# Scan stage of an eight-layer kernel: the second block's depthwise convolution on TensorE with diagonal tap matrices instead of on VectorE

## The reference, cut to what matters

```
xc, z  = split(x @ in_proj.T)
xt     = depthwise_conv(xc, conv_w, 4 taps, causal, zeros ahead of each sequence) + conv_b
xs     = silu(xt)
dt, B, C = split(xs @ x_proj.T);  dt = softplus(dt @ dt_proj.T + dt_b)
h[t]   = exp(dt[t] * A) * h[t-1] + dt[t] * B[t] * xs[t]        # per channel and state
y      = (sum over states of h * C + D * xs) * silu(z)
out    = y @ out_proj.T
```

## Time and profile before

| what | value |
|---|---|
| median of 3 runs | 4525.6 us (4520.05 to 4526.73) |
| the profiled execution, own time | 4532.35 us |
| its span in the trace | 4530.6 us |
| busy: PE, DVE, ACT, POOL | 3978.4, 3387.8, 2843.7, 2065.0 us |
| scan stage starts (input norm rows) | about 1639 us |
| step 0: first scan to first scan of step 1 | 1676.05 to 1839.87 us |

### The profile page before, as it was taken

The page is one execution under the profiler, slowest core; times in us unless marked ns, Lnnn a source line. Parts: engine busy times, 40 slices in busy tenths (PEclk is TensorE's granted clock), DMA queues, the critical chain, the costliest instruction groups (busy, mean ns, idle before and its releaser), DMA issues. The chain is left out here.

```text
span 4530.6 us, 106618 instructions
## 1 busy us (share of the span) xinstructions
PE 3978.4 (88%) x39260; PEld 2174.0 (48%) x39268; DVE 3387.8 (75%) x5857; ACT 2843.7 (63%) x4508; POOL 2065.0 (46%) x1885
## 2 busy tenths in 40 slices
PE   8899999887859842599999999999988999999888
PEld 4344444554637520244545445455453555555555
DVE  8899999565654469888888888885146888888586
ACT  3577777554443236688887888875124666667664
POOL 5122222331224559888888788885011222222312
PEclk9899999889978975799999999999998999999999
DMA  4211111015324434355555655654223212222100
GB/s 137 64 37 39 36 37 39 12 43 114 62 98 122 108 108 104 104 164 143 150 159 153 163 138 150 174 149 130 83 74 103 70 55 58 57 65 59 31 10 29
DMA packets 263622, 411.22 MB, mean 91 GB/s; under 512 B 52636, under 2 KB 139708, under 8 KB 263076
## 3 DMA queue, kind: packets, MB, share of 16 engines
q1 hardware_dynamic: 233480, 376.07, 29.4%
q0 software_dynamic: 6912, 18.88, 1.7%
q10 hardware_dynamic: 22848, 11.02, 1.2%
HBM read 351.85 MB, written 53.24 MB: 89 GB/s over the span
## 5 line engine op out<-in xcount | busy, mean ns | idle before, releaser
L992 DVE CUSTOM_DVE_ANT_0 banks<-banks,l3s_table 128x1024 f32<-128x1024 f32 x512 | 620.0, 1240 | 126.9 <-PE banks L912 121.7
L1073 ACT ACTIVATE l3s_probs<-banks 128x512 f32<-128x512 f32 x1024 | 542.4, 595 | 256.3 <-PE banks L912 139.0
L2688 POOL TENSOR_TENSOR l_dbx<-l_u,l_bc 128x1024 f32<-128x1024 f32 x256 | 602.8, 2355 | 178.6 <-DVE l_u L3093 62.0
L987 DVE TENSOR_REDUCE l0s_peak<-banks 128x1 f32<-128x1024 f32 x512 | 604.7, 1212 | 59.5 <-PE banks L912 59.1
L1073 ACT ACTIVATE l0s_probs<-banks 128x512 f32<-128x512 f32 x1024 | 536.1, 600 | 174.1 <-PE banks L912 172.4
L2698 POOL TENSOR_TENSOR l_ys<-l_ys,l_hc 128x1024 f32<-128x1024 f32 x232 | 547.3, 2359 | 40.7 <-DVE l_hc L3113 36.4
L2929 ACT ACTIVATE banks<-l_dt,l_decay 128x512 f32<-128x512 f32 x512 | 345.4, 686 | 218.7 <-DVE banks L3102 215.5
L2826 PE MATMUL banks<-l_ha,l_ring 128*128 128x512 f32 x1024 | 446.6, 593 | 0.1
L2826 PE MATMUL banks<-l_hb,l_ring 128*128 128x512 f32 x1024 | 442.9, 593 | 1.6 <-DMA l_ring<-in_l2f_stream 1.6
L912 PE MATMUL banks<-l3s_q_st,l3s_k_st 122*32 122x512 bf16 x4096 | 359.5, 385 | 32.4 <-issue 22.4
L3102 DVE TENSOR_TENSOR_SCAN banks<-banks,l_carry,l_dbx 128x512 f32<-128x512 f32 x256 | 329.4, 1288 | 76.0 <-ACT banks L2929 49.5
(11 more groups left out here) (499 smaller groups left out, 7271.8 us busy)
## 6 DMA issues: line engine op xcount, KB each, us to landing
l_bc<-l_bc_rows SPq DMA_DIRECT2D x256, 512.0 KB, 5.3
l_ring<-in_l2f_stream SPq DMA_DIRECT2D x176, 512.0 KB, 6.5
l3s_table<-bias_table SPq DMA_DIRECT2D x16, 960.0 KB
y_rows<-l1f_out_b SPq DMA_DIRECT2D x80, 128.0 KB
qk_parts<-l0q_q_parts SPq DMA_DIRECT2D x48, 128.0 KB
qk_parts<-l0q_k_parts SPq DMA_DIRECT2D x48, 128.0 KB, 2.4
l0s_q_st<-qk_parts SPq DMA_DIRECT2D x64, 96.0 KB
l0s_k_st<-qk_parts SPq DMA_DIRECT2D x64, 96.0 KB
```

Source lines behind the costliest of these rows:

```text
L987: nc.vector.tensor_reduce(out=peak[:, b % 2, t:t + 1], in_=s1[t % 2], axis=AX, op=ALU.max, negate=True).then_inc(s1_used, 1)
L992: nc.vector.tensor_tensor_reduce(out=s1[t % 2], in0=s1[t % 2], in1=rows, scale=1.0, scalar=LOW, op0=ALU.add, op1=ALU.max, accum_out=peak[: ...
L1073: nc.scalar.activation(columns(probs[b % 2][:, t, :], half * 512, (half + 1) * 512), scores, ACT.Exp, scale=scale).then_inc(s2_used, 1)
L2688: nc.gpsimd.tensor_tensor(dbx[:, at:at + 2], u[:, 2 * mh:2 * mh + 2], bc[:, load % BR, 0].unsqueeze(1).to_broadcast([P, 2, TB]), ALU.mult)\
```

## The change

The convolution of block 1 alone, whose input is taken in step 0, is made by TensorE. In the prologue, between taking the turned rows and `take_x(0, 0)`, ScalarE builds 16 matrices of 128x128 float32 (four taps, four channel groups), each the identity scaled per row by a tap. They lie in `ha`, which the perceptron fills only from step 1 on. In step 0, TensorE, after the four input projections and ahead of the projection to dt, B and C, makes four matmuls of 128x512 per group, one per tap, with the diagonal as the stationary matrix and the shifted `xc` as the moving one, accumulating in the group's bank. `take_x` for block 1 is then the copy alone; the bias goes into silu's own bias operand. VectorE makes no convolution in step 0; the reset of the first three columns moves from behind unit 42 to behind unit 46, ahead of `gated`, with a wait for the four convolutions. Blocks 0 and 2 to 7 are as before.

```diff
+        diagonals = ha[:, 0:TAPS, :].rearrange("p j (c m) -> p j c m", m=P)
...
+            def convolve_second(c):
+
+                bank = place[f"in1.{c}"][0]
+                pe.wait_ge(tap_done, CT + c + 1)
+                for j in range(TAPS):
+                    last = nc.tensor.matmul(banks[:, bank, :], diagonals[:, j, c, :], xc[:, c, j:j + TB],
+                                            start=(j == 0), stop=(j == TAPS - 1))
+                last.then_inc(conv_ready, 1)
...
+                    if q == AT["xp_pe"] and n == 0:
+                        pe.wait_ge(diagonals_ready, 1)
+                        for c in range(CT):
+                            convolve_second(c)
                     if q == AT["xp_pe"] and more:
                         project_dbl(n + 1)
...
+                if n == 1:
+                    nc.scalar.activation(xc[:, i, TAPS - 1:], banks[:, bank, :], ACT.Copy).then_inc(tap_done, 1)
+                    return
                 nc.scalar.activation(xc[:, i, TAPS - 1:], banks[:, bank, :], ACT.Copy)
...
-                nc.scalar.activation(xs[n % 2][:, i, :], banks[:, bank, :], ACT.Silu).then_inc(taken[bank], 1)
+                offset = {"bias": conv_b[:, i:i + 1]} if n == 1 else {}
+                nc.scalar.activation(xs[n % 2][:, i, :], banks[:, bank, :], ACT.Silu, **offset).then_inc(taken[bank], 1)
...
             act.wait_ge(first_loaded, 16 * 3)
+            for j in range(TAPS):
+                for c in range(CT):
+                    last = nc.scalar.activation(diagonals[:, j, c, :], chip.ident[:], ACT.Copy, scale=taps[:, c, j:j + 1])
+            last.then_inc(diagonals_ready, 1)
             for i in range(CT):
                 take_x(0, i)
...
                     for i in range(CT):
-                        if k == AT["conv"][i] and more:
+                        if k == AT["conv"][i] and n and more:
                             convolve(n + 1, i)
+                    if n == 0 and k == AT["xs"][CT - 1]:
+                        v.wait_ge(conv_ready, 2 * CT)
+                        nc.vector.memset(xc[:, :, 0:TAPS - 1], 0.0).then_inc(xc_kept, 1)
```

More of the change, by code:

```diff
@@ L2491, in scan_and_mlp @@
         tap_done, conv_ready, xc_kept = s.sem("tap_done"), s.sem("conv_ready"), s.sem("xc_kept")
+        diagonals_ready = s.sem("diagonals_ready")
         skip_done = s.sem("skip_done")
```

## The result

The changed kernel takes 4538.3 us (median of 13 runs, 4533.3 to 4542.1) against 4526.7 us for the kernel before on the same chip (13 runs, 4520.1 to 4529.5). The ratio is 1.0026, 95% interval 1.0018 to 1.0033. It is 12 us slower where 3 us faster was forecast, and the forecast range ended at 4531. The profiled execution took 4538.82 us, its span is 4537.0.

The account below looks back on a forecast made before the run. GpSimd was taken to bound step 0, with VectorE limiting only beside convolutions. Step 0's -4.0 us and the prologue's +0.8 gave -3.2, from 4525.6 to a median of 4522.4 us, range 4514 to 4531.

Parts of the forecast that it names:

- What bounds step 0: Step 0: GpSimd sets the pace, 4.61 us per pair against VectorE's 3.95; its 6.32 us of idle pieces can be had.
- Term A: Step 0: GpSimd's gaps waiting for a scan or product by C close once VectorE's convolutions go, gaining 4.0 us.
- The gap at `gated` stays: End of step 0: GpSimd's 2.46 us gap remains, as VectorE operations with two SBUF inputs and GpSimd's take turns.
- Term B: Prologue: ScalarE's 16 diagonals take 4.67 us where 3.88 are free, so `take_x(0, 0)` starts 0.8 us late.
- B counts in full: Prologue: the 0.8 us delay from building diagonals passes wholly to the first scan, as everything up to it hangs on `take_x(0, 0)`.
- TensorE's cost 0: Step 0: convolution groups of 4.4 to 8.1 us delay silus too little to matter; cost 0, bounds 0 and 5 us.
- VectorE's waits for GpSimd: Step 0, units 30 to 46: VectorE's idle time before scans grows from one 0.70 us wait to 5 to 6 us.
- Later steps are as before: After step 0: nothing changes; diagonals are read before step 1 writes `ha`, GpSimd and transfers keep their order.
- the change touches only these 200 us: Start of prediction: only the 200 us holding prologue and step 0 are affected; what they gain or lose passes on.
- a slower time for a reason that no row shows: Whole kernel: a slower outcome from a cause not visible in the profile rows, chance 0.03.

Follow-up runs that it names:

- k = 16: Kernel before plus 16 tiny bf16 matmuls on TensorE ahead of block 1's first projection, VectorE's convolution kept: 4546.7 us against 4536.1, ratio 1.0024.

## Why the prediction was wrong, step by step

**What bounds step 0: right.** GpSimd did, and its idle pieces were what could be had. With VectorE freed by 9.7 us the step gains 3.8.

**Term A, -4.0 us: right, -3.77.** The product behind `gated` was forecast at 1790.6, it came at 1790.58 (shifted). All 3.86 us of gaps closed. Later 0.28 us is lost at one scan that waits 1.44 us for its exponential, before 1.16. Over all traces step 0 takes 163.8 us with VectorE's convolution (163.79 to 163.85, nine traces) and 159.8 to 160.1 with TensorE's (six).

**The gap at `gated` stays: right.** It is 2.46 us as before, although VectorE reaches its multiplication earlier: at 1779.32, 0.2 us before GpSimd starts its add at 1779.52. It now takes 3.63 us in place of 2.23 and ends 1.1 us behind that add (1781.87). The two take turns.

**Term B, +0.8 us: right at the copy, wrong in what it costs.** The 16 diagonals took 4.78 us where 4.67 were forecast, and the first copy of `xc` comes 0.79 us late. But "B counts in full" did not hold. VectorE's convolution ends 0.56 us late, then TensorE's last products of the projection to dt, B and C are done so much sooner (ScalarE waits 1.19 us for them in place of 1.75), and the first scan is not late at all in this pair. From first projection to first scan the five kernels with diagonals in the prologue take 31.40 to 31.46 us and the ten others 31.04 to 31.46, on average 0.2 us less. The granted clock in the last 2.5 us ahead of that copy is 0.84 in place of 0.78, which fits; why it is higher is open. The scan stage alone would have given -3.8, not -3.2.

**TensorE's cost 0: right.** The groups took 3.60 to 6.37 us, and the third silu starts 8.52 us behind its copy's end, as before. Three scans wait 0.2, 1.2 and 0.2 us for an exponential behind a silu; GpSimd shows no gap there, so they cost nothing.

**VectorE's waits for GpSimd: mis-sized.** I forecast one wait of 0.70 us to grow to 5 to 6 us. Four waits of 0.67 to 0.78 came, 3.0 us, and 1.6 us for ScalarE.

**"Later steps are as before": this is the step that failed.** It was argued from data and order: same instructions, same waits, same transfers. The same assumption stands at the start of the prediction, "the change touches only these 200 us". It left out that 65 instructions more stand in TensorE's stream, so that all later code of that engine lies elsewhere against the packets in which it is fetched. In a loop of 3912 instructions this moved the end of the first packet behind each back-jump from 83 to 18 instructions. That cost 2.7 us a pass, 13.7 in all, over three times the gain. The profile of the kernel before had the sign: "PE banks L912 <- issue" with five waits of over 4 us, in a loop with five back-jumps. I had read the profile only near the change. I had given 3 in 100 to a slower time for a reason that no row shows; a row did show where such a reason could act.

What is shown and what is not: that position alone makes and unmakes the loss is shown, by the same loss without convolution, by its absence with padding, and by its absence without jumps. That the second packet is late, and not something else at the same instruction, rests on the place of the stall, which moves with the padding instruction for instruction (18, 20, 52), and on the trace's own record of each packet. At all 60 back-jumps of the twelve kernels that have them, a packet of 16 KB lands 1.5 to 1.8 us ahead of TensorE's resumption. The next one starts to move only 0.4 to 1.6 us after the resumption. At all 20 second stalls it is this one that lands 1.2 to 1.7 us ahead of their end. At the second jump of the changed kernel: stop at 3711.28, packet from 3713.05 to 3714.01, resumption at 3715.66, next packet from 3717.30 to 3718.26, end of the second stall at 3719.58. Why one pass of the kernel with k = 16 fetched 19 packets, and why 16 matmuls inside the loop did not make it 18 in each pass, is open.

## What to carry to other kernels

An edit is not local if it changes the number of an engine's instructions ahead of a long hardware loop. Look for "issue" waits that recur once a pass, and in the records of instruction packets for one that lands shortly ahead of each resumption, and compare with a padded copy before believing that a change of 0.3% comes from what it does; here padding alone moved the kernel by 0.2%. Where each pass of such a loop starts with a stall, try writing it out on that engine: it was worth 32 us here, eight times what the change gains in the scan stage.

## What the hardware showed that was not expected

- A back-jump of TensorE over 3912 instructions costs 4.2 to 5.8 us of standstill (2.6 to 4.3 with the table moved earlier) and, with the half clock behind it, 6.6 us a pass in the kernel before. The same stream without jumps is fetched with no visible stall.
- Behind a jump the second packet starts to move only 0.4 to 1.6 us after TensorE has resumed, and its instructions start 2.8 to 4.0 us after the resumption. A loop with 18, 20 or 52 instructions in its first packet paid again; with 83 and more it did not. Where between 52 and 83 the limit lies was not measured.
- Behind a jump TensorE shows 1.2 GHz. Where it then stood still a second time (k = 16, second jump, 1.2 us), it made 72 matmuls in the first 8 us in place of 108.
- A 960 KB load ahead of small urgent ones cost TensorE 2.1 to 2.9 us in the middle of each pass; behind them, it cost some 1.6 us at each jump.
